# Loading block numbers into TensorE's registers eight at a time instead of sixteen at a time

## The reference, cut to what matters

```python
edge_index = jnp.stack([src, dst])
h = jnp.maximum(_layernorm(x), 0.0); x = x + _L0_gnn_ref(h, edge_weight, ...)            # weighted mean of neighbours
h = jnp.maximum(_layernorm(x), 0.0); x = x + _L1_gnn_ref(h, ..., edge_attr_64, ...)      # rows times edge attributes
h = jnp.maximum(_layernorm(x), 0.0); x = x + _L2_gnn_ref(h, edge_index, ...)             # GATv2 attention, 5 heads
h = jnp.maximum(_layernorm(x), 0.0); x = x + _L3_gnn_ref(h, edge_index, edge_type_8, ...) # relational attention, 8 types
# each step gathers h[src], forms one message per edge, and adds the messages up by dst:
h_neigh = jax.ops.segment_sum(msg, dst, num_segments=n)
```

## Time and profile before

| | us |
|---|---|
| median of the timed runs (2 runs) | 9897.29 (9896.61 to 9897.97) |
| span of the profiled execution | 11974.2 |
| TensorE matmul busy in it | 7534.2 (63%) |
| VectorE busy | 7367.7 (62%) |
| GpSimd busy | 5383.2 (45%) |
| ScalarE busy | 2310.3 (19%) |

### The profile page before, as it was taken

The page is one execution under the profiler, slowest core; times in us unless marked ns, Lnnn a source line. Parts: engine busy times, 40 slices in busy tenths (PEclk is TensorE's granted clock), DMA queues, the critical chain, the costliest instruction groups (busy, mean ns, idle before and its releaser), DMA issues. The chain is left out here.

```text
span 11974.2 us, 162471 instructions
## 1 busy us (share of the span) xinstructions
PE 7534.2 (63%) x38295; PEld 5244.5 (44%) x38296; DVE 7367.7 (62%) x10447; ACT 2310.3 (19%) x8712; POOL 5383.2 (45%) x5649
## 2 busy tenths in 40 slices
PE   2878788667677775555548555554855554855557
PEld 1666566555555552333347323333732222622226
DVE  6665433355555555677799567778955555745558
ACT  0222344300000001111159111114910000000000
POOL 2555555455545543665400266550015553055550
PEclk9888888788878885777755577775557666867768
DMA  2333344344444444766649566664933333333333
GB/s 60 87 84 84 99 114 114 90 113 111 110 95 113 111 96 163 234 233 231 194 203 411 179 232 232 229 216 173 415 120 74 74 73 63 116 72 75 75 72 100
DMA packets 851293, 1717.47 MB, mean 143 GB/s; under 512 B 384638, under 2 KB 473541, under 8 KB 796922
## 3 DMA queue, kind: packets, MB, share of 16 engines
q1 hardware_dynamic: 465500, 1137.96, 27.5%
q0 software_dynamic: 207456, 413.40, 15.8%
q10 hardware_dynamic: 178256, 165.14, 4.1%
HBM read 1263.59 MB, written 453.99 MB: 143 GB/s over the span
## 5 line engine op out<-in xcount | busy, mean ns | idle before, releaser
L556 POOL DMA_INDIRECT gathered_rows<-node_table,index x2496 | 2379.1, 953 | 2000.0 <-issue 652.4
L719 PE MATMUL ps_G<-table_parts,low_onehots 125*128 125x320 bf16 x15600 | 2712.0, 336 | 294.1 <-issue 220.8
L576 PE MATMUL ps_sum<-messages,onehots 128*125 128x65 f32 (+3 forms) x13312 | 2113.4, 321 | 993.1 <-issue 643.6
L576 PEld LDWEIGHTS ps_sum<-messages,onehots 128*125 128x125 f32 x13312 | 2011.7, 236 | 1117.9 <-issue 1111.2
L556 POOL DMA_INDIRECT gathered_rows<-xl_table,index x1664 | 1576.7, 948 | 1828.5 <-issue 1028.0
L556 POOL DMA_INDIRECT gathered_rows<-rel_table,index x1456 | 1391.9, 956 | 2009.8 <-ACT index L546 1020.9
L1524 PE MATMUL ps_Z<-xr,onehots_wide 125*128 x3328 | 1505.3, 610 | 1194.5 <-issue 628.4
L719 PEld LDWEIGHTS ps_G<-table_parts,low_onehots 125*128 125x128 bf16 x15600 | 1677.7, 110 | 1183.2 <-issue 312.8
L749 DVE TENSOR_TENSOR rows_by_feature<-ps_G,fifth_onehots 128x320 f32<-128x320 f32 x1040 | 507.0, 487 | 2271.9 <-remote 1683.0
L1524 PEld LDWEIGHTS ps_Z<-xr,onehots_wide 125*128 125x128 f32 x3328 | 801.4, 257 | 1899.3 <-issue 1802.7
L1572 DVE TENSOR_TENSOR z<-gathered_rows,ps_Z 128x650 f32<-128x650 f32 x832 | 670.9, 828 | 835.4 <-issue 499.7
(11 more groups left out here) (326 smaller groups left out, 7209.2 us busy)
## 6 DMA issues: line engine op xcount, KB each, us to landing
stash_a<-gathered_rows SPq DMA_DIRECT2D x208, 1300.0 KB
kept_rows<-stash_a SPq DMA_DIRECT2D x208, 1300.0 KB
onehots<-onehots_kept SPq DMA_DIRECT2D x520, 500.0 KB
onehots_turned<-onehots_turned SPq DMA_DIRECT2D x416, 250.0 KB
stash_r<-gathered_rows ACTq DMA_DIRECT2D x208, 272.0 KB
kept_rows<-stash_r SPq DMA_DIRECT2D x208, 272.0 KB
low_rows<-low_rows SPq DMA_DIRECT2D x416, 125.0 KB
onehots_kept<-onehots ACTq DMA_DIRECT2D x104, 500.0 KB
```

Of the source, the lines that this page charges most:

```text
L556: pool.indirect_dma_start(G[:, HALF * k + q, 0:width], None, table, bass.IndirectOffsetOnAxis(IDX[:, k, q:q + 1], 0)).then_inc(gathered[k] ...
L576: return nc.tensor.matmul(ps_sum[0:BN, bass.ds(at, width)], S[:, j, :], M, start=False, stop=True, skip_group_check=True)
L719: last = nc.tensor.matmul(ps_G[:, (fetch * k + g) % 2, 0:D * FIVE], OT[0:BN, k, g, a, :], HP[:, part, a, :, :].rearrange("p f b -> p (f b) ...
```

## The change

At all six places 8 numbers are loaded at each group in place of 16 at every second one. A pass has 104 loads of 8 values in place of 52 of 16. The number of values loaded is the same. The constant PAIR goes. The indices into `at` follow.

```diff
-PAIR = 2 * HALF
@@ weighted_sums, turn
-                                if k % 2 == 0:
-                                    at = blocks_of(i * U + HALF * k, PAIR, places[0:1, :], ...)
+                                at = blocks_of(i * U + HALF * k, HALF, places[0:1, :], ...)
...
-                                    last = sum_chunk(ps_sum, S, j, M[:, j, :], D + 1, at[j % PAIR])
+                                    last = sum_chunk(ps_sum, S, j, M[:, j, :], D + 1, at[j % HALF])
@@ attribute_sums and relation_scores, turn
-                                if k % 2 == 0:
-                                    at = blocks_of(i * U + HALF * k, PAIR)
+                                at = blocks_of(i * U + HALF * k, HALF)
@@ pair_scores
-                                if m % 8 == 0:
-                                    at = blocks_of(i * U + 2 * m, PAIR)
+                                if m % 4 == 0:
+                                    at = blocks_of(i * U + 2 * m, HALF)
@@ shared_sums
-                                    if q == 0 and h % 2 == 0:
-                                        at = blocks_of(HALF * (HT * i + h), PAIR)
+                                    if q == 0:
+                                        at = blocks_of(HALF * (HT * i + h), HALF)
```

More of the change, by code:

```diff
@@ L903, in turn @@
                                 n = K * i + k
-                                if k % 2 == 0:
-                                    at = blocks_of(i * U + HALF * k, PAIR, places[0:1, :], (NB - 1) * (D + 1) + (NB - 1) // PER * (BANK - PER * (D + 1)))
+                                at = blocks_of(i * U + HALF * k, HALF, places[0:1, :], (NB - 1) * (D + 1) + (NB - 1) // PER * (BANK - PER * (D + 1)))
                                 if not hist:
@@ L1055, in turn @@
                                 for j in range(HALF * k, HALF * (k + 1)):
-                                    last = sum_chunk(ps_sum, S, j, M[:, j, :], D, at[j % PAIR] * D)
+                                    last = sum_chunk(ps_sum, S, j, M[:, j, :], D, at[j % HALF] * D)
                                 last.then_inc(chunk_done.sem, HALF)
@@ L1524, in _ @@
                                     last = nc.tensor.matmul(ps_Z[:, m % 2, q, 0:PW], SW[0:BN, j % WIDE, :],
-                                                            XR[:, bass.ds(at[j % PAIR] * PW, PW)], start=True, stop=True)
+                                                            XR[:, bass.ds(at[j % HALF] * PW, PW)], start=True, stop=True)
                                 last.then_inc(dest_made.sem, 1)
@@ L1705, in turn @@
                                     last = nc.tensor.matmul(ps_Q[:, q // QH, q % QH * QW:(q % QH + 1) * QW], ST[0:BN, j, :],
-                                                            XQ[:, bass.ds(at[j % PAIR] * QW, QW)], start=True, stop=True)
+                                                            XQ[:, bass.ds(at[j % HALF] * QW, QW)], start=True, stop=True)
                                 last.then_inc(dest_made.sem, 1)
@@ L1961, in _ @@
                                         pe.wait_ge(own_copied.sem, own_copied.at(HT * i + h + 1))
-                                    sum_chunk(ps_sum, S, j, M[:, j, :], out_w, at[j % PAIR] * P).then_inc(chunk_done.sem, 1)
+                                    sum_chunk(ps_sum, S, j, M[:, j, :], out_w, at[j % HALF] * P).then_inc(chunk_done.sem, 1)
                         nc.tensor.matmul(ps_sum[:, 6 * BANK + 3 * P:7 * BANK], zero[:, 0:P], zero[:, 0:P], start=False, stop=True,
```

## The result

| | before | after |
|---|---|---|
| median of the timed runs (2 each), us | 9897.29 | 10146.03 (10139.15 to 10152.91) |
| span of the profiled execution, us | 11974.2, a second one 9897.4 | 10151.1 |

The change makes the kernel slower: ratio 1.0251, 95% interval 1.0234 to 1.0267, 249 us more. The forecast was 9864, the range 9790 to 9950.

What follows compares the result with a forecast made beforehand. No engine was full; TensorE was taken as bound only in the short shared sums. Savings of 25.5, 11 and 8 us, less some 5 back, gave 40 off 11974, scaled to 9864 us timed; range 9790 to 9950.

Steps and rivals of the forecast that it cites:

- The load's size: TensorE's address loads: one of 8 values costs about 575 ns, by a line through 16 and 4 values.
- The rival that goes by the instruction: All passes: a load of 8 also costs 1107 ns, exposures come once more, 64 us slower, 9950 timed; chance 0.12.
- The added 110 us of sequencer time, hidden: TensorE's sequencer: 624 more loads at about 0.18 us each, lying under the array's queued work.
- TensorE: 197 of 216 us, so it is the bound: Short shared sums: TensorE is the bound, VectorE at 192 leaves room, so all 25.5 us of array waits count.
- the slower rival: Load time goes by instruction, 1107 ns each: 9950 timed; slower by 2% only from 0.38 us a load; chance 0.12.
- The 22.5 us and the 16 us of the weighted and attribute passes: Exposed gaps: 22.5 us in the second weighted, 16 us in first weighted and attribute passes; half counted, 11 and 8.
- Pair, relation and long shared passes unchanged: These passes gain nothing: loads are covered by the gather, the picks and the DMA engines.
- Moved standstills: Attribute passes: rival that long array standstills shift with instruction placement, some 416 us (3.5%) gone or doubled; chance 0.05.
- The scaling of all terms by 17%: Whole kernel: timed runs are 17% below the profiled span, so the saving was taken as the same share.
- More exposed than the profile shows: Six TensorE-heavy passes: rival that 312 loads each stand out 0.5 us more, 156 us gained, 9768 timed; chance 0.06.
- The 25.5 us at L576 near zero: Short shared sums: sign that the array's waits at L576 after L1922, 25.5 us, nearly vanish in the profile after.
- The short shared sums near 203 us: Short shared sums: sign that the profile after shows them near 203 us instead of 216.

Runs made afterwards that it cites:

- short16: The changed kernel with only the two short shared passes put back to loads of 16 at every second group; 9899.02 us, ratio 1.0001.
- before_again: The kernel before, unchanged, profiled a second time; 9899.16 us, span 9897.4.
- short8: The kernel before with loads of 8 in the two short shared passes alone; 10138.76 us, ratio 1.0248.
- fewwaits16: The kernel before without two of the three waits at each group of the short passes; 9863.44 us, ratio 0.9961.
- warm: The changed kernel with one more matmul of zeros ahead of each group of the short passes; 9933.47 us, ratio 1.0037.
- wait1: The kernel before with one more, already satisfied wait ahead of each group in the short passes; 10144.32 us, ratio 1.025.

## Why the prediction was wrong, point by point

**The load's size: right.** Forecast 575 ns, measured 592. With 1107 for 16 and 2133 for 32 a load on TensorE costs about 64 ns a value and 80 ns; ScalarE's 309 for 4 is near that line. The two pair passes are the exception, told at the end. The rival that goes by the instruction fell, although the sign of the result was its own: it wanted 1107 ns a load and a loss in three kinds of passes. 592, 1107 and 2133 ns for 8, 16 and 32 show that the time goes by the count.

**The added 110 us of sequencer time, hidden: right in ten passes, wrong in two.** short16 has 520 of the 624 added loads and stands at 1.0001. In the short passes nothing was hidden: the sum had 0.18 us for each new load, 0.36 a turn, and 0.49 us a turn came out in full, 8.12 to 8.61 us.

**"TensorE: 197 of 216 us, so it is the bound": the step that failed.** From it came the largest term of the sum, 25.5 us less in the short passes; they became 247 us longer. The 197 busy us at full clock were read as the array's own need. The array needs 7.10 us a turn, or less, and was given 8.12. Part of the spare time was hidden where the profile counts the array as busy: 7.55 us for 64 records against 7.10 for the same 64 behind a full queue. A record lasts 273 ns (L576 of before_again), while behind a full queue one begins every 111 ns (7.10 / 64), so by my estimate some 0.16 us of every stop in their starts shows as busy; two stops a turn and the gaps of 0.55 and 0.15 us make 7.10 + 0.32 + 0.70 = 8.12. The engine was at its limit, but with its sequencer, where the change put more work. So the gap of 0.57 us was not the load's exposed remainder, to vanish with a shorter load. In short8, with the load over half a microsecond sooner, it is still 0.51; in fewwaits16, with the loads of before and fewer waits, it is 0.19.

**The clock as a constant: the second failure, and nine times the larger.** The sum priced every microsecond of the array at the clock of the earlier trace rows, 0.99 in the short pass. Nothing in it allowed the change to move the clock, and no rival did either. Of the 249 us some 25 are sequencer time, by short8's turns; the rest is the fall to half clock. A price per load (the slower rival put the point of "slower by 2%" at 0.38 us a load, and so out of reach) cannot see such a step: 104 loads of 592 ns brought 2.5%.

**The 22.5 us and the 16 us of the weighted and attribute passes: not gained.** short16 keeps loads of 8 in these passes and has the time of before, so the 19 us that I counted weren't there. The likely reason is in the waits of GpSimd in the first weighted pass, which the array's busy share of 80% hid; for after:

```profile
L555 POOL DMA_INDIRECT gathered_rows<-node_table,index x619: 940/944/962, 217.1 to 988.7; - x155
...
POOL gathered_rows L555 <- issue: 156.0, 512, 0.3
```

619 gathers follow one another in 771.6 us, 1.25 us each: 0.944 of work and 0.3 between, with next to nothing waited for. That is the length of the pass. That the gathers pace it is read from the rows; it wasn't tried.

**Pair, relation and long shared passes unchanged: right**, by the rows at the top and by short16.

**Moved standstills: fell**, as the prediction thought likelier. They are gone in the second profile of the same kernel. The scaling of all terms by 17% was wrong for the largest of them: the array's waits at L576 after L1922 are 25.5 us in the long execution and 25.7 in the undisturbed one. And I should have doubted the bounds read from an execution that ran 21% long: the weighted pass has the array 80% busy in the earlier trace rows and 91% (703 of 773 us) in the undisturbed one. **More exposed than the profile shows: fell**, by short16's 1.0001 and the longer short passes.

**The signs it named.** "The 25.5 us at L576 near zero" came true (1.1 us idle in the pass), for the opposite reason. "The short shared sums near 203 us" was the sign that told: 339. A sign that counts idle time is worth nothing without the clock beside it.

## What to carry to other kernels

Where matmuls are short (111 ns a record here) and each has its own address from a register, count the sequencer's instructions per turn (loads, waits even if satisfied, register operations, the branch) and compare the turn's length with that of the same matmuls behind a full queue; a busy share above 90% (197 of 216 us here) doesn't say which of the two is the bound. A change that lengthened such a turn by 6% (8.12 to 8.61 us) cost the array half its clock here (0.50), so put the granted clock of the stretch into the sum as a term of its own. And profile again before predicting when the span is far above the timed runs.

## What the runs showed of the hardware

- The clock did not come back under load. In after the array worked without a gap for 300 us at a granted clock of 0.50, and the same matmuls hold full clock in before for 215 us (0.99). The clock stood at 1.00 after the 14 matmuls of 512 columns at the head of a short pass (8372 to 8388 in after). In every profile in which a short pass lost it, full clock had lasted at most 48 us (in short8 it was 1.00 from 8366 to 8413), and it did not return in that pass. Gaps of 0.46 to 0.96 us between groups stood ahead of each fall. But gaps of 0.55 us stand in before too, where the clock held (0.99 over the pass).
- One bf16 matmul with 384 columns of zeros a group (0.17 us to the start of the next in warm, 8402.58 to 8402.75), at a cost of 20 us a pass, held the clock and saved 213 us of 10146.
- A wait that is already satisfied isn't free. Two of them taken off each of a turn's four groups cut it from 8.12 to 7.35 us, 0.10 us each; four added in wait1 cost 0.11 us each. In the second execution of before the three waits of a group start 0.1 us apart (L1959 to L1961: 8411.4, 8411.5, 8411.6) and last 32 to 36 ns each.
- A load takes far longer in the pair passes. In the first of them, DMA share 0.90, a load of 8 takes 2576 ns in the median (after):

```profile
L526 PEldq TENSOR_LOAD <-rows x95: 1977/2576/3236, 3706.8 to 4647.1; - x95
```

and one of 16 takes 3698 ns (before):

```profile
L527 PEldq TENSOR_LOAD <-rows x48: 3222/3698/4159, 3707.8 to 4647.0; - x48
```

Busy DMA engines alone are not the cause: in the first long shared pass, DMA share 0.99, a load of 16 takes its 1106 ns (before).

```profile
L527 PEldq TENSOR_LOAD <-rows x52: 1102/1106/1129, 4895.2 to 5362.0; - x52
```

In the long execution of before, too, with the first pair pass at a DMA share of 0.70, the median is 1108 ns, so the earlier trace rows didn't show it. What slows the loads stays open. Two loads of 8 there take 1.45 us more than one of 16, not the 0.08 us of the other passes, and it is hidden all the same.
